# A hand-written plan for four engines: feed-forward jobs at fixed distances, and VectorE's rounding work in six units instead of three

## The reference

```
x  = inputs                       # (4, 1024, 128), float32
xn = layernorm(x)
# attention, 16 heads of 8 columns
q, k, v = xn @ Wq + bq, xn @ Wk + bk, xn @ Wv + bv      # split in heads
scores  = q k^T / sqrt(8) + slope[h] * (key position - last position)
attn    = softmax(scores) @ v @ Wo + bo
# feed-forward, 128 -> 352 -> 128
fp4(t)  = every block of 16 along the last axis, divided by max|t| / 6,
          rounded to 0, .5, 1, 1.5, 2, 3, 4, 6, and multiplied back
gate    = fp4(xn) @ fp4(w_gate)^T
up      = fp4(xn) @ fp4(w_up)^T
h       = silu(gate) * up                                # 352 columns
ffn     = fp4(h) @ fp4(w_down)^T
out     = x + attn + ffn
```

## Time and profile before

| | |
|---|---|
| median of 3 runs | 860.6 us (858.37 to 861.62) |
| the profiled execution | 858.46 us, of which 856.7 us are the span of its instructions |
| PE busy | 778.5 us, 91% of the span |
| DVE busy | 695.4 us, 81% |
| ACT busy | 652.2 us, 76% |
| POOL busy | 416.5 us, 49% |
| mean granted clock of PE | 0.961 of full speed |

### The profile page before, as it was taken

One profiled execution on the slowest core, in us unless ns is written; L12 is line 12 of the kernel. 1 busy time (PEld: TensorE's weight loads), 2 busy tenths in 40 slices (PEclk: granted clock), 3 DMA queues, 4 the chain that ended last, 5 costly groups with the idle time before them and its releaser, 6 DMA issues.

```text
span 856.7 us, 13894 instructions
## 1 busy us (share of the span) xinstructions
PE 778.5 (91%) x4939; PEld 232.0 (27%) x4939; DVE 695.4 (81%) x792; ACT 652.2 (76%) x1342; POOL 416.5 (49%) x413
## 2 busy tenths in 40 slices
PE   3289998989999999899899999999999999998986
PEld 2012232223232333222232333222222323232322
DVE  7797886888989897788888887888888898989710
ACT  4206886878888888778788888887888888888885
POOL 7365263482628373662545462761717362442442
PEclk9657998999999999989999999999999999999999
DMA  5920002013102010050101011050102000000000
GB/s 149 243 51 1 2 2 76 2 50 100 39 1 51 2 67 10 14 149 1 39 2 38 3 45 45 2 160 2 38 2 50 3 14 2 2 1 2 2 2 25
DMA packets 32828, 31.85 MB, mean 37 GB/s; under 512 B 4344, under 2 KB 26552, under 8 KB 32760
## 3 DMA queue, kind: packets, MB, share of 16 engines
q1 hardware_dynamic: 32760, 30.96, 13.4%
HBM read 15.91 MB, written 15.04 MB: 36 GB/s over the span
## 4 chain that ended last, share of the span: by engine, by line
PE 66%; DVE 17%; ACT 6%; POOL 6%; issue 3%; DMA 1%; SPq 0%; POOLq 0%; ACTq 0%; DVEq 0%
PE low L1078 23%; PE mx L1048 21%; DVE neg_max L934 13%; PE low L1067 6%; ACT probs L728 4%; PE low L1116 3%; PE low L1101 2%; PE low L1095 2%; PE low L1034 2%; PE mx L1127 2%; PE low L1108 2%; ACT pv_s L825 1%; POOL mb L537 1%; DVE am L905 1%; PE low L1030 1%
## 5 line engine op out<-in xcount | busy, mean ns | idle before, releaser
L934 DVE TENSOR_REDUCE neg_max<-mx 128x1 f32<-128x1024 f32 x512 | 614.1, 1220 | 99.5 <-PE mx L1048 91.4
L728 ACT ACTIVATE probs<-low 128x512 f32<-128x512 f32 x1024 | 558.7, 607 | 141.1 <-PE low L1067 135.2
L1048 PE MATMUL mx<-k_op,q_op 51*128 51x512 bf16 x1024 | 320.1, 398 | 42.0 <-DVE neg_max L934 21.8
L1067 PE MATMUL low<-q_op,k_op 53*128 53x512 bf16 x1024 | 334.4, 389 | 12.7 <-ACT probs L728 9.1
L1078 PE MATMUL low<-probs,v_op 128*32 128x512 f32 x2048 | 275.7, 611 | 0.3
L1048 PEld LDWEIGHTS mx<-k_op,q_op 51*128 51x128 bf16 x1024 | 61.8, 95 | 318.2 <-issue 171.5
L1067 PEld LDWEIGHTS low<-q_op,k_op 53*128 53x128 bf16 x1024 | 74.7, 93 | 91.6 <-ACT probs L728 81.9
L630 POOL CAST neg_parts<-neg_max 128x16 bf16<-128x16 f32 x31 | 6.8, 219 | 167.1 <-DVE neg_max L934 102.1
L537 POOL TENSOR_SCALAR mb<-mb 128x960 f32<-128x960 f32 (+2 forms) x17 | 58.7, 3456 | 27.5 <-DVE mb L925 26.2
L1078 PEld LDWEIGHTS low<-probs,v_op 128*32 128x32 f32 x2048 | 40.5, 108 | 67.5 <-issue 32.2
L618 POOL TENSOR_TENSOR x_s<-x_s,down_s 128x128 f32<-128x128 f32 x32 | 14.6, 455 | 80.5 <-ACT down_s L761 57.9
(11 more groups left out here) (128 smaller groups left out, 589.8 us busy)
## 6 DMA issues: line engine op xcount, KB each, us to landing
q_op<-q_rows SPq DMA_DIRECT2D x32, 192.0 KB, 3.8
k_op<-k_rows SPq DMA_DIRECT2D x32, 192.0 KB, 4.8
q_rows<-qp SPq DMA_DIRECT2D x8, 384.0 KB, 2.6
k_rows<-kp SPq DMA_DIRECT2D x8, 384.0 KB, 2.9
x_s<-in_L_attn_inputs_dram SPq DMA_DIRECT2D x8, 256.0 KB, 3.8
q_rows<-qp SPq DMA_DIRECT2D x8, 256.0 KB, 2.9
k_rows<-kp SPq DMA_DIRECT2D x8, 256.0 KB, 3.1
out_dram<-o_s SPq DMA_DIRECT2D x8, 256.0 KB, 2.6
```

The lines of the kernel that those rows point to most:

```text
L728: nc.scalar.activation(probs[U % 3][:, 2 * g + x, :], bank("exp", U, j), ACT.Exp).then_inc(st_free, 1)
L934: nc.vector.tensor_reduce(to, slot("max", pos)[:], AX.X, ALU.max, negate=True).then_inc(mx_free, 1)
L1048: ins = nc.tensor.matmul(slot("max", pos)[:, 512 * kh:512 * kh + 512], q, k, start=True, stop=True)
L1067: nc.tensor.matmul(bank("exp", U, j), k_op[quad][r, g, kt * P:(kt + 1) * P], q_op[quad][r, g, half * HALF:(half + 1) * HALF], start=True, ...
```

## The change

The constants and the planner change, and the offsets at which DVE and POOL do the steps of rounding:

```diff
-FFN_FIRST, FFN_LAST = 5, 237
+FFN_FIRST, FFN_LAST = 6, 229
-ROUNDED = 10
+FROM_XT = {("gate", 0): 1, ("gate", 1): 3, ("up", 0): 10, ("up", 1): 11, ("hT", 0): 21, ("hT", 1): 27,
+           ("down", 0): 28, ("down", 1): 29}
+ROUNDED = 12
 def plan():
...
-    x_at = put(FFN_FIRST, "xT", 0)
     for p in range(NP):
-        U = put(x_at + 1, "gate", p, 0)
-        U = put(U + 1, "gate", p, 1)
-        U = put(U + 2, "up", p, 0)
-        up = put(U + 1, "up", p, 1)
-        U = put(up + ROUNDED, "hT", p, 0)
-        U = put(U + 1, "hT", p, 1)
-        if p + 1 < NP:
-            x_at = put(FFN_FIRST + (FFN_LAST - FFN_FIRST) * (p + 1) // (NP - 1), "xT", p + 1)
-        U = put(U + 1, "down", p, 0)
-        put(U + 1, "down", p, 1)
+        start = FFN_FIRST + (FFN_LAST - FFN_FIRST) * p // (NP - 1)
+        U = put(start, "xT", p)
+        for kind in ("gate", "up", "hT", "down"):
+            if kind == "hT":
+                U += ROUNDED - 1
+            for t in range(2):
+                U = put(max(U + 1, start + FROM_XT[kind, t]), kind, p, t)
     for b in range(1, B):
         for g in (2 * b, 2 * b + 1):
-            U = norm_unit(b) + 1 + 8 * (g % 2)
+            U = norm_unit(b) + 1 + 4 * (g % 2)
...
     for hb in range(2 * B):
-        U = put(at["pvT", hb // 2 * 8 + 6 + hb % 2] + 1, "ctxT", hb)
+        U = put(max(U, at["pvT", hb // 2 * 8 + 6 + hb % 2], at["down", 2 * hb + 1, 1] - 1) + 1, "ctxT", hb)
         for i in range(2):
-            U = put(max(U, at["down", 2 * hb + 1, 1]) + 1, "wo", hb, i)
+            U = put(max(U, at["down", 2 * hb + 1, 1]) + 1 + i, "wo", hb, i)
# POOL
-                    if U == up + 3:
+                    if U == up + 5:
                         scale_to_grid(p + 1)
-                    if U == up + 5:
+                    if U == up + 7:
                         add_power(p + 1)
-                    if U == up + 7:
+                    if U == up + 9:
                         take_power(p + 1)
-                    if U == up + 8:
+                    if U == up + 10:
                         scale_back(p + 1)
# DVE; i is 0 or 1, the reduction of the unit behind which the step stands
-                        if (U, i) == (up0 + 2, 0):
+                        if (U, i) == (up0 + 2, 1):
                             hidden_maxima(p + 1, 0)
-                        if (U, i) == (up1 + 2, 0):
+                        if (U, i) == (up1 + 2, 1):
                             hidden_maxima(p + 1, 1)
-                        if (U, i) == (up1 + 2, 1):
+                        if (U, i) == (up1 + 3, 1):
                             block_scales(p + 1)
-                        if (U, i) == (up1 + 3, 0):
+                        if (U, i) == (up1 + 4, 1):
                             block_inverses(p + 1)
-                        if (U, i) == (up1 + 4, 1):
+                        if (U, i) == (up1 + 6, 1):
                             powers(p + 1)
```

More of the change, by code:

```diff
@@ L147, in plan @@
             put(max(U, QUADS * UNITS * (b - 1) + 2) + 1, "v", g)
+    U = 0
     for hb in range(2 * B):
-        U = put(at["pvT", hb // 2 * 8 + 6 + hb % 2] + 1, "ctxT", hb)
+        U = put(max(U, at["pvT", hb // 2 * 8 + 6 + hb % 2], at["down", 2 * hb + 1, 1] - 1) + 1, "ctxT", hb)
         for i in range(2):
-            U = put(max(U, at["down", 2 * hb + 1, 1]) + 1, "wo", hb, i)
+            U = put(max(U, at["down", 2 * hb + 1, 1]) + 1 + i, "wo", hb, i)
     return at
```

## The result

| | before | after |
|---|---|---|
| median, six runs each on one chip | 861.3 us (858.4 to 862.8) | 869.2 us (865.2 to 871.8) |
| ratio of the runs, 95% interval | | 1.009 (1.0063 to 1.0117) |
| again, on another chip | 857.3 us | 864.8 us, 1.0077 (1.0048 to 1.0105) |
| profiled execution, span | 856.7 us | 869.9 us |
| marker of unit 2 to marker of unit 255 | 767.15 us | 775.00 us |

A forecast was written before the change was run, and what follows sets the result against it. Bound taken: a loop of ACT's exponentials, banks and PE's scores and value product, plus 19 us of PE waits. Removed 19, added 17.8 + 0.6 + 0.3 + 4.2 = 22.9: 3.9 above 860.6, so 864.5 us, range 853 to 873.

The forecast's parts named there:

- The waits at `hT`: PE stands ahead of hT for POOL's late chain in eleven pairs; 17.8 us in all, 13 to 22.
- the chain with `swish` and `max_parts`: POOL's queue from add_power to hT: 10.27 us, plus 3.75 for swish and 0.7 for max_parts.
- Removed: PE's waits for rounding steps on DVE and POOL, largest at units 20 and 93 to 96, go: 19 us.
- DVE's steps in job units: Rounding steps moved into units with a middle job, where DVE has room, cost 0 (bounds 0 and 0.1 a step).
- The small wait of DVE at unit 93: The second hidden_maxima still waits for hidden in POOL's order: some 0.3 us, a new small cost.
- The clock: PE drops to its lower clock behind the waits of pairs 4 and 11: 2.1 us each, 4.2 (bounds none and 8.4).
- the copy: One more copy of the value product falls in a job unit: + 0.3 us.
- Rival 1: PE makes up the waits at hT in the job units behind; 17.8 becomes 2.6, total 849 us; chance 0.15.
- Rival 2: Waits at hT bring no lower clock, or are somewhat shorter; 860.3 us, no change; chance 0.21.
- rival 5: DVE's steps in job units cost 0.1 each after all, 7.5 for 75 steps; 872 us; chance 0.05.
- Rival 3: Two further clock drops (pairs 5, 10) or longer waits, 4.2 us each way; 868.7, both 872.9; chance 0.15.
- Rival 4: Every one of the eleven waits at hT brings a clock drop, nine more by 2.1; 883 us; chance 0.04.

The follow-up runs named there:

- swish late: Changed kernel with swish three units later in POOL's queue, four units behind gate 1, after scale_back; 841.1 us, 0.980 of before.
- after again: The changed kernel, unaltered, run once more on another chip; 864.8 us, 7.5 above before there.
- long filler: Kernel of swish late plus three zero-fills of a dead tile on POOL ahead of every take_power but the first; 862.0 us, 1.006 of before.
- offsets alone: Plan from before the change with ROUNDED 12, keeping the changed offsets of DVE's and POOL's steps; 856.1 us, 0.997 of before.
- mask earlier: Changed kernel with the mask (powers) and add_power each one unit earlier; 856.3 us, 0.998 of before.
- plan alone: Changed plan, with all nine offsets of DVE's and POOL's steps put back to those before; 847.2 us, 0.987 of before.
- free copies: Kernel of swish late, with feed-forward jobs, ctxT and wo kept off units 8n + 1; 837.3 us, 0.977 of before.

## Why the prediction was right, and where it was too small

**The waits at `hT`: right, pair by pair.** Lateness as worked out, against PE's idle ahead of `hT` in the profile after:

| pair | 0 | 1 | 2 | 4 | 5 | 6 | 9 | 10 | 11 | 12 | 13 | 3, 7, 8, 14, 15 |
|---|---|---|---|---|---|---|---|---|---|---|---|---|
| forecast | 0.5 | 1.5 | 1.7 | 3.5 | 2.0 | 1.5 | 1.3 | 2.4 | 3.7 | 1.5 | 1.5 | 0 |
| measured | 0.41 | 0.85 | 1.85 | 3.62 | 2.17 | 1.23 | 1.07 | 2.33 | 3.91 | 1.48 | 1.23 | 0 |

21.1 forecast, 20.1 measured. The terms hold too: the mask ended 2.10 after its marker, as the earlier trace rows has it; the chain with `swish` and `max_parts`, 748.57 to 763.33, took 14.8, where 10.27 + 3.75 + 0.7 is 14.7. The unit with `hT` gives 0.35 back, not 0.3. That makes the cost 16.2; 17.8 was forecast.

**Removed: right.** By the prediction's own lengths of the units, 20.3 us are left over in the units 3 to 255 before. About 1.4 of that are hundredths, at the turns above all (1.2 in swish late), and 18.8 us are waits with their drops of the clock, where 19 was taken. DVE's steps in job units cost nothing (swish late has a unit longer than its kind by over 0.3 nowhere but at 96). The small wait of DVE at unit 93 is 0.75 rather than 0.3, and that unit is no longer for it. But small delays of 0.2 to 0.4 at units 24, 44, 96, 117, 203 and 221 occurred; with others they make 1.9 instead of 0.6.

**The clock: the term that was too small.** I counted two drops at 2.1, 4.2 us. There were five, behind the waits of pairs 2, 4, 5, 10 and 11 (1.85, 3.62, 2.17, 2.33, 3.91), and what these units lost beyond the waits sums to 8.2, about 1.6 a drop (1.4 to 1.9), not 2.1. Four drops was the upper bound, so their number was beyond it, their cost just within it (8.4). The step that was off is the reading of the earlier trace rows: I took a wait of 2.40 with a drop and one of 1.24 without for a border near the former. The size depends on the execution: after again has four drops with the same waits, and by the same reckoning they cost 4.9, 0.7 more than forecast.

16.2 + 8.2 + 1.9 + 0.3 (the copy) - 18.8 is 7.8, against 7.85 by the markers. That is 4 more than forecast: 4.0 more for the clock and 1.3 more for small delays, less 1.6 for the waits. These are two single executions. The median moved by the same 7.9 on that chip and by 7.5 on the other, but the second profile of after is only 4.6 longer than before's by the markers, so that the close agreement of 7.85 with the median may be partly luck. What is not: the waits of single pairs, equal in both profiles of after, and that both chips show the kernel slower by 0.8 to 0.9%.

**The rivals.** Rival 1 (waits made good afterwards) is out: each unit gave back its 0.35 and none behind it anything, and the filler brings the loss back. Rival 2 (no lower clock) is out, as is rival 5. Rival 3, more drops, is what happened, though its longer waits did not. Rival 4, a drop at each of the eleven waits, is out as well: the waits of 0.85 to 1.48 brought none in either profile of the kernel. The Trainium skill, TensorE: Matmul & The Clock Gate, section "HAM oscillation — how this bites in real kernels", on which rival 4 drew, tells of waits of some 3 to 5 us, each with a drop behind it. Here every wait of 3 us or more (3.12 to 3.92, in both profiles of after and in the long filler) had one behind it too, but so had shorter ones, down to 1.69, which are not the section's case.

## What to carry to other kernels

When a plan moves steps of one engine to make room on it, write out the queue of every other engine that takes part, with the position of each foreign step between, and compare it to the time that the waiting engine takes to arrive: here `swish`, which nobody had touched, fell between two steps of the rounding, and its 3.75 us turned a gain of 17 us into a loss of 8. A step that waits for another engine's progress (`max_parts`) resets the queue behind it: starting the chain ahead of it earlier gained 0.07 us in pair 5. In this kernel a wait on TensorE cost its length less 0.35 and, from 1.7 us on, mostly a stretch at the lower clock behind it, 0.9 to 1.9 us more; where waits of about 2 us recur, count the clock for each, and expect the count to differ between executions.

## What had not been expected of the hardware

**The lower clock comes behind waits shorter than thought, and not every time.** Drops followed idle stretches of PE of 1.69 (offsets alone, unit 196), 1.83 (mask earlier, unit 157), 1.85 (after), 2.10, 2.17, 2.32 and more. None followed 1.98 in mask earlier (unit 177), 2.35 in offsets alone (unit 72), nor the same 1.85 in the second profile of after. Behind a single wait of 1.53 or less none was seen. So between 1.7 and 2.4 it is open, for the same kernel, from one execution to the next. One of the cases without, its value product at the higher level (PE of mask earlier):

```profile
615.66 0.52 PE L1108 MATMUL low<-ident,hq 128*128 128x128 f32 x3 [1.98 <-POOLq L565]
616.65 1.06 PE L1078 MATMUL low<-probs,v_op 128*32 128x512 f32 x8
```

And one drop came without such a wait. In the second profile of swish late the clock falls at unit 250, among free units near the end, where PE stood 0.53 once in each of the units ahead and never longer. The same units ran at the higher level in the other thirteen profiles. The granted clock is 0.50 from 815 to 818, and it costs 1.5:

```profile
814.52 0.54 PE L1067 MATMUL low<-q_op,k_op 53*128 53x512 bf16 x1 [0.26 <-ACT probs L728]
814.99 1.93 PE L1078 MATMUL low<-probs,v_op 128*32 128x512 f32 x8
```

**A DVE instruction of 0.17 us that took 3.64.** Ahead of unit 2, DVE splits the maxima of the first half by an addition of two SBUF tiles, 16 columns. Timeline of before, then of after, with POOL's `take_power` beside it:

```profile
58.91 3.66 POOL L543 TENSOR_TENSOR zb<-zb,mb 128x1632 f32<-128x1632 f32 x1
58.91 0.18 DVE L938 TENSOR_TENSOR neg_parts<-neg_max,neg_parts 128x16 bf16<-128x16 f32 x1
```

```profile
61.41 3.62 POOL L543 TENSOR_TENSOR zb<-zb,mb 128x1632 f32<-128x1632 f32 x1
61.41 3.64 DVE L938 TENSOR_TENSOR neg_parts<-neg_max,neg_parts 128x16 bf16<-128x16 f32 x1
```

Both engines' instructions start together in each profile. Where DVE's is short, POOL's is 0.04 longer; where it is long, it lasts as long as POOL's. It looks as if one of the two had to wait for the other; that the first to start is the one that goes on is a guess. The Trainium skill, GPSIMD Engine Reference, section "1. Specifications", has the SBUF interfaces of the two engines shared, with contention from DVE instructions that read two SBUF inputs; the rows agree as far as they go. PE waits 2.95 for this at its `turn`; with 2.5 us by which its first chunk of scores comes later it makes the 5.4 by which the profile after starts later. The long case is in the profiles of after and of plan alone, the short one in those of the other kernels and of after again, so it is not of the change. I tried to settle the order by a wait of POOL, in the kernel with free copies:

```diff
             add_power(0)
+            pool.wait_ge(parts_max_ok, 1)
             take_power(0)
```

> The kernel with free copies, and POOL waits ahead of its first take_power until DVE has split the maxima of the first half (a DVE addition with two inputs from SBUF, 16 columns). In the profiles of before and of six other kernels this addition took 0.17 to 0.18 us and started together with take_power, in those of the changed kernel and of the plan alone it took 3.64, as long as take_power beside it. Theory (which of the two engines comes first is open at that point, and DVE has to wait for POOL where POOL is first): the wait settles it, the long case never comes; median 0 to 1.5 below that of the kernel with free copies on this chip, and fewer executions some 3 us above it. Rival (the long case has another cause): same median, same spread.

It gave 838.1 (835.7 to 838.4) beside 836.1 (835.7 to 838.6) without the wait: no gain and no narrower spread, as the rival has it. The long case stands in neither profile, so that its share in the spread of the medians, and its cause, stay open.

The 2.5 us have a like pair of rows. At 13.23 DVE casts 16 partitions of `probs` (L880) while POOL fills tiles. Before, then after:

```profile
13.23 1.05 DVE L880 CAST probs<-probs 16x1024 bf16<-16x1024 f32 x1
13.68 1.49 POOL L504 MEMSET q_op<- 128x1024 f32 x1
```

```profile
13.23 3.73 DVE L880 CAST probs<-probs 16x1024 bf16<-16x1024 f32 x1
13.69 0.94 POOL L504 MEMSET q_op<- 128x1024 f32 x1
```

Where the cast is short, POOL's fill beside it takes 0.55 longer; where it is long, it ends 0.55 behind POOL's last fill (16.41). What it writes goes out by DMA ahead of the rows of k in the same queue, and PE's first chunk waits for these: it starts at 37.98 before and at 40.47 after. The cast is short in two of the fourteen profiles, of before and of swish late, whose unit 2 has its marker at 77.5 and 77.0; in the other twelve it took 3.73, and unit 2 comes at 79.0 to 79.8, or at 82.9 and 83.5 where the addition is long too. Swish late has it short once and long once, so this is not of the change either. It is why the lengths from marker to marker are compared here and not the spans. In the middle of the kernel it can be seen once more: in after, L914 on DVE takes 1.15 instead of 0.19 at 368.73, beside `three_parts` on POOL and just ahead of the 0.4 lost at unit 96. What decides the order no run shows.
